# A new slot table behind the attention scores, and a tail whose last batch is finished tile by tile

## The reference

```
def _L0_attn_ref(x, w_in, b_in, w_out, b_out):          # 16 heads of 16
    x_proj = (x @ w_in.T + b_in).reshape(b, l, h, -1)
    q, k, v = jnp.split(x_proj, 3, axis=-1)
    att = jnp.einsum('blhd,bmhd->blmh', q, k) * scale
    att = jax.nn.softmax(att, axis=2)
    opt = jnp.einsum('blmh,blhd->blhd', att, v).reshape(b, l, d)
    return opt @ w_out.T + b_out
...
x = x + _layernorm(_L0_attn_ref(_layernorm(x), ...))
x = x + _layernorm(_L0_ffn_ref(_layernorm(x), ...))
```

## Time and profile before

| what | value |
|---|---|
| median of three runs | 593.8 us (593.7 to 595.99) |
| profiled execution: time, span | 595.68 us, 593.9 us |
| PE, weight loads, DVE, ACT, POOL busy | 519.8, 414.0, 489.3, 466.8, 211.3 us |
| share of the span | 88, 70, 82, 79, 36% |
| exponentials (L358) | 512, idle before them 16.5 us |
| maxima (L499) | 512, idle before them 36.9 us, mostly for PE |
| mean granted clock of PE | 0.94 of full speed |

### The profile page before, as it was taken

How to read it: one execution, slowest core, us unless ns; L and a number is a source line. 1 busy time by engine, 2 the same in 40 slices (tenths; PEclk the granted TensorE clock), 3 DMA queues, 4 the chain that set the end, 5 groups by cost and what they waited for, 6 DMA issues and landing times.

```text
span 593.9 us, 8508 instructions
## 1 busy us (share of the span) xinstructions
PE 519.8 (88%) x2640; PEld 414.0 (70%) x2640; DVE 489.3 (82%) x1025; ACT 466.8 (79%) x1249; POOL 211.3 (36%) x385
## 2 busy tenths in 40 slices
...
GB/s 255 13 238 168 74 117 94 0 130 84 94 13 125 76 55 100 84 70 62 142 24 120 72 108 35 143 71 72 35 140 73 57 54 2 1 36 0 1 36 35
DMA packets 21812, 46.16 MB, mean 78 GB/s; under 512 B 4901, under 2 KB 13221, under 8 KB 21128
## 3 DMA queue, kind: packets, MB, share of 16 engines
...
## 4 chain that ended last, share of the span: by engine, by line
PE 42%; DVE 26%; ACT 21%; POOL 6%; issue 2%; SPq 1%; DMA 0%; POOLq 0%; DVEq 0%; ACTq 0%
PE pu L148 23%; ACT ps L358 16%; DVE nmax L499 14%; PE ps L163 9%; DVE st L529 5%; PE ps L148 4%; POOL y L720 2%; PE pu L168 2%; DVE inter L525 2%; POOL nmr L714 2%; DVE mv L534 2%; ACT inter L421 2%; PE pu L254 1%; ACT vo L378 1%; DVE qk L513 1%
## 5 line engine op out<-in xcount | busy, mean ns | idle before, releaser
L358 ACT ACTIVATE ps<-ps,nmax 128x512 f32<-128x512 f32 x512 | 341.5, 680 | 16.5 <-DVE nmax L499 16.2
L499 DVE TENSOR_REDUCE nmax<-ps 128x1 f32<-128x512 f32 x512 | 322.3, 681 | 36.9 <-PE ps L163 35.9
L163 PE MATMUL ps<-stack 128*128 128x512 f32 x512 | 196.9, 457 | 24.8 <-ACT ps L358 18.5
L163 PEld LDWEIGHTS ps<-stack 128*128 128x128 f32 x512 | 98.5, 203 | 73.8 <-ACT ps L358 55.4
L358 ACT ACTIVATION_READ_ACCUMULATOR ps<-ps,nmax 128x1 f32 x512 | 116.2, 227 | 0.0
L148 PE MATMUL pu<-yT,wi_r 128*128 128x512 f32 x336 | 90.2, 404 | 6.1 <-DVE inter L525 4.8
L148 PEld LDWEIGHTS pu<-wo_r,inter 128*128 128x128 f32 x624 | 80.8, 190 | 5.1 <-DVE qk L513 1.4
L148 PE MATMUL pu<-wo_r,inter 128*128 128x256 f32 x624 | 84.2, 285 | 0.0
L148 PEld LDWEIGHTS pu<-yT,wi_r 128*128 128x128 f32 x336 | 63.0, 191 | 23.1 <-DVE inter L525 6.4
L711 POOL TENSOR_SCALAR nmr<-mv 128x4 f32<-128x4 f32 (+1 forms) x35 | 8.4, 239 | 156.4 <-DVE mv L534 155.8
L734 POOL TENSOR_TENSOR ml<-gs,g 128x128 f32<-128x128 f32 x8 | 3.3, 413 | 146.6 <-DVE g L616 146.6
...
## 6 DMA issues: line engine op xcount, KB each, us to landing
stack<-qk SPq DMA_DIRECT2D x256, 128.0 KB, 2.5
...
```

Of the source, the lines that this page charges most:

```text
L163: e.matmul(ps[i % NS][:], st[:, 1 - p, c, t * 128:(t + 1) * 128], st[:, 2, c, :], start=True, stop=True).then_inc(scored, 1)
L358: e.activation(ps[i % NS][:], ps[i % NS][:], ACT.Exp, bias=nmax[:, i % 8:i % 8 + 1], accum_out=ssum[:, b % 2, t, h:h + 1]).then_inc(exped, 1)
L499: e.tensor_reduce(nmax[:, i % 8:i % 8 + 1], ps[i % NS][:], AX_X, ALU.max, negate=True).then_inc(maxed, 1)
```

## The change

All three slot tables are written anew. In batch b, `f1` units 0 to 2 of batch b - 1 now stand at the end (PE slots 29 to 31), and units 3 to 7 of batch b - 2 at slots 0 to 2, 7 and 8. `masked_t` moves from slot 31 to 28 on PE and from slot 0 of the next batch to slot 28 on ACT. The four projection tiles stand in two slots instead of four; `f2` is split into slots 10 to 13 and 24 to 27; in the last batch (b = 7) it fills slots 9 to 17 instead (`g` and `h` choose: the one that is out of range issues nothing). On Pool `y2_norm` goes ahead of `x_norm`. In the tail five `f1` units of batch 6 are left, two of them behind the projections; Pool does both first passes before both second ones. The last batch's second layer is one unit per tile in a bank of its own, with copy, statistics, norm, add and store tile by tile. The diff, cut to its core (indentation halved; old table lines mostly left out, since they are printed above):

```diff
@@ -97,7 +97,7 @@
 bg_loaded, wout_loaded, lora_loaded, rows_moved = sem("bg_l"), sem("wout_l"), sem("lora_l"), sem("rows_m")
...
 stacked = [sem(f"stacked{i}") for i in range(PIECES)]
-stored = [sem(f"stored{i}") for i in range(XB + 1)]
+stored = [sem(f"stored{i}") for i in range(XB)]
...
@@ -112,6 +112,7 @@
 xnT_high, qk_high, yT_high, f1_high = (sem(n + "_high") for n in ("xnT", "qk", "yT", "f1"))
...
 v_here, oT_here, y_here, gT_here, lt_here, y2_here = (sem(n + "_here") for n in ("v", "oT", "y", "gT", "lt", "y2"))
+f2_tile_ps, y2_tile_here, tile_stored = sem("f2_tile_ps"), sem("y2_tile_here"), sem("tile_stored")
...
@@ -268,6 +269,15 @@
         if k:
...
           filling.clear()
+
+  def f2_last(t):
+
+    bank = banks[take(("f2", B - 1, t), y2_tile_here, t + 1)]
+    if t == 0:
+      e.wait_ge(f1_low, 8 * B)
+    three(bank[:, 0:256], lambda a, f: inter[:, a, f, t * 128:(t + 1) * 128], lambda a, f: wo_r[:, a, f, :],
+       range(8), True, False)
+    e.matmul(bank[:, 0:256], ones_r[:], br_r[:, BW], start=False, stop=True).then_inc(f2_tile_ps, 1)
...
@@ -287,61 +297,62 @@
       e.wait_ge(wout_loaded, 16)
...
       e.wait_ge(lora_moved, 16)
-    slot(0), f1(b - 2, 0)
-    slot(1), f1(b - 2, 1)
-    slot(2), f1(b - 2, 2)
+
+    g, h = (b - 2, B) if b < B - 1 else (B, b - 2)
+    slot(0), f1(b - 2, 3)
+    slot(1), f1(b - 2, 4)
+    slot(2), f1(b - 2, 5)
     slot(3), o_t(b - 1, 0), o_t(b - 1, 1)
-    slot(4), f1(b - 2, 3)
...
-    slot(31), masked_t(b - 1)
+    slot(4)
+    slot(5), project(b - 1, 0), project(b - 1, 1)
+    slot(6), project(b - 1, 2), project(b - 1, 3)
+    slot(7), f1(b - 2, 6)
+    slot(8), f1(b - 2, 7)
+    slot(9), x_t(b + 1, 0), x_t(b + 1, 1), f2(h, 0, 0)
+    slot(10), f2(g, 0, 0), f2(h, 0, 1)
+    slot(11), f2(g, 0, 1), f2(h, 1, 0)
+    slot(12), f2(g, 1, 0), f2(h, 1, 1)
+    slot(13), f2(g, 1, 1), f2(h, 2, 0)
+    slot(14), q_k(b + 1, 0), f2(h, 2, 1)
+    slot(15), q_k(b + 1, 1), f2(h, 3, 0)
+    slot(16), y_t(b - 1, 0), y_t(b - 1, 1)
+    slot(17), q_k(b + 1, 2), f2(h, 3, 1)
+    slot(18), q_k(b + 1, 3)
+    slot(19), gate(b - 1)
+    slot(20), value(b + 1, 0)
+    slot(21), value(b + 1, 1), gate_t(b - 1)
+    slot(22), value(b + 1, 2)
+    slot(23), value(b + 1, 3)
+    slot(24), f2(g, 2, 0)
+    slot(25), f2(g, 2, 1)
+    slot(26), f2(g, 3, 0)
+    slot(27), f2(g, 3, 1)
+    slot(28), masked_t(b - 1)
+    slot(29), f1(b - 1, 0)
+    slot(30), f1(b - 1, 1)
+    slot(31), f1(b - 1, 2)
   b = B - 1
...
     banks.append(ps[i])
-  for f in range(4):
-    f1(b - 1, f)
+  f1(b - 1, 3), f1(b - 1, 4)
   o_t(b, 0), o_t(b, 1)
-  for f in range(4, 8):
-    f1(b - 1, f)
+  f1(b - 1, 5)
   for t in ALL:
     project(b, t)
-  f2(b - 1, 0, 0), f2(b - 1, 0, 1), f2(b - 1, 1, 0), f2(b - 1, 1, 1)
+  f1(b - 1, 6), f1(b - 1, 7)
+  f2(b - 1, 0, 0), f2(b - 1, 0, 1), f2(b - 1, 1, 0)
   y_t(b, 0), y_t(b, 1)
+  f2(b - 1, 1, 1)
+  gate(b)
   f2(b - 1, 2, 0)
-  gate(b)
-  f2(b - 1, 2, 1)
   gate_t(b)
-  f2(b - 1, 3, 0), f2(b - 1, 3, 1)
+  f2(b - 1, 2, 1), f2(b - 1, 3, 0), f2(b - 1, 3, 1)
   masked_t(b)
...
   for t in ALL:
-    f2(b, t, 0), f2(b, t, 1)
+    f2_last(t)
...
@@ -438,56 +449,59 @@
       pair(PAIRS * b + s)
...
       e.wait_ge(bg_loaded, 16)
-    slot(0), masked_t(b - 2)
-    slot(1), f1(b - 2, 0)
-    slot(2), f1(b - 2, 1)
-    slot(3), f1(b - 2, 2)
+    g, h = (b - 2, B) if b < B - 1 else (B, b - 2)
+    slot(0), f1(b - 2, 2)
+    slot(1), f1(b - 2, 3)
+    slot(2), f1(b - 2, 4)
+    slot(3), f1(b - 2, 5)
     slot(4), o_t(b - 1, 0), o_t(b - 1, 1)
-    slot(5), f1(b - 2, 3)
...
-    slot(20)
+    slot(5)
+    slot(6), project(b - 1, 0)
+    slot(7), project(b - 1, 1)
+    slot(8), f1(b - 2, 6)
+    slot(9), f1(b - 2, 7)
+    slot(10), x_t(b + 1, 0)
+    slot(11), x_t(b + 1, 1)
+    slot(12)
+    slot(13), f2(h, 0)
+    slot(14), f2(g, 0)
+    slot(15), q_k(b + 1, 0)
+    slot(16), q_k(b + 1, 1)
+    slot(17), y_t(b - 1, 0), y_t(b - 1, 1)
+    slot(18), q_k(b + 1, 2), f2(h, 1)
+    slot(19), q_k(b + 1, 3)
+    slot(20), gate(b - 1)
     slot(21)
-    slot(22), gate(b - 1)
...
-    slot(28)
+    slot(22), logits(b - 1)
+    slot(23), gate_exp(b - 1)
     if b == 0:
       e.wait_ge(late, 16)
-    slot(29), value(b + 1, 0)
-    slot(30)
-    slot(31), value(b + 1, 1)
+    value(b + 1, 0)
+    slot(24)
+    slot(25), value(b + 1, 1)
+    slot(26)
+    slot(27)
+    slot(28), masked_t(b - 1)
+    slot(29), f2(g, 1)
+    slot(30), f1(b - 1, 0)
+    slot(31), f1(b - 1, 1)
   b = B - 1
-  masked_t(b - 1)
-  for f in range(4):
-    f1(b - 1, f)
+  f1(b - 1, 2), f1(b - 1, 3), f1(b - 1, 4)
   o_t(b, 0), o_t(b, 1)
-  for f in range(4, 8):
-    f1(b - 1, f)
+  f1(b - 1, 5)
   project(b, 0), project(b, 1)
+  f1(b - 1, 6), f1(b - 1, 7)
+  y_t(b, 0), y_t(b, 1)
   f2(b - 1, 0)
-  y_t(b, 0), y_t(b, 1)
   gate(b), logits(b), gate_exp(b)
...
     f1(b, f)
-  f2(b, 0), f2(b, 1)
+  e.wait_ge(added[3], 4 * b)
+  for t in ALL:
+    e.wait_ge(f2_tile_ps, t + 1)
+    e.activation(y2[:, t, :], bank_of["f2", b, t][:, 0:256], ACT.Copy).then_inc(y2_tile_here, 1)
...
@@ -529,7 +543,7 @@
     e.bn_stats(st6[n][:, t, :], src[:, t, :]).then_inc(stats[i], 1)
...
   def whole_stats(i, n, b, ts):
-    e.wait_ge(stats[i], 8 * b + (4 if ts[0] else 0) + len(ts))
+    e.wait_ge(stats[i], 8 * b + 2 * ts[0] + len(ts))
...
@@ -616,7 +630,7 @@
       e.tensor_tensor(g8[:, 5], g8[:, 4], wide(4), ALU.is_equal).then_inc(gated, 1)
...
   def norm(i, n, dst, src, b, ts):
-    e.wait_ge(rstd[i], 3 * b + 3 if ts[0] == 0 else 3 * b + 6)
+    e.wait_ge(rstd[i], 3 * b + 3 + 3 * (ts[0] // len(ts)))
     for t in ts:
...
               ALU.mult).then_inc(normed[i], 1)
@@ -649,56 +663,63 @@
   for b in range(B):
...
       pair(PAIRS * b + s + 1)
-    slot(0), ratio(b - 1)
...
-    f1(b - 2, 2), slot(4)
+    g, h = (b - 2, B) if b < B - 1 else (B, b - 2)
+    f1(b - 2, 1), slot(0), ratio(b - 1)
+    f1(b - 2, 2), slot(1)
+    f1(b - 2, 3), slot(2)
+    f1(b - 2, 4), slot(3), x_stats(b + 1)
+    f1(b - 2, 5), slot(4)
     slot(5)
-    f1(b - 2, 3), slot(6)
...
-    y_t(b - 1, 0), y_t(b - 1, 1), slot(21)
+    slot(6)
+    slot(7), y_stats(b - 1, HALVES[0])
+    slot(8), y_stats(b - 1, HALVES[1])
+    f1(b - 2, 6), slot(9)
+    f1(b - 2, 7), slot(10)
+    slot(11)
+    x_t(b + 1, 0), x_t(b + 1, 1), slot(12), sum_stats(b - 1)
+    slot(13)
+    slot(14), y2_stats(h, HALVES[0])
+    slot(15), y2_stats(g, HALVES[0])
+    slot(16)
+    q_k(b + 1, 0), slot(17)
+    q_k(b + 1, 1), slot(18)
+    y_t(b - 1, 0), y_t(b - 1, 1), slot(19), y2_stats(h, HALVES[1])
+    q_k(b + 1, 2), slot(20)
+    q_k(b + 1, 3), slot(21)
     slot(22)
-    slot(23)
...
-    slot(31)
+    gate_1(b - 1), slot(23)
+    slot(24), gate_2(b - 1)
+    slot(25), gate_3(b - 1)
+    slot(26)
+    slot(27)
+    slot(28)
+    slot(29)
+    slot(30), y2_stats(g, HALVES[1])
+    f1(b - 1, 0), slot(31)
   b = B - 1
+  f1(b - 1, 1)
   ratio(b)
-  for f in range(8):
+  for f in range(2, 6):
     f1(b - 1, f)
   y_stats(b, HALVES[0]), y_stats(b, HALVES[1])
-  for ts in HALVES:
-    norm(1, 1, y, y, b, ts), add(1, y, b, ts)
-    sum_stats(b, ts)
+  norm(1, 1, y, y, b, HALVES[0]), add(1, y, b, HALVES[0])
+  f1(b - 1, 6)
+  sum_stats(b, HALVES[0])
+  f1(b - 1, 7)
+  norm(1, 1, y, y, b, HALVES[1]), add(1, y, b, HALVES[1])
+  sum_stats(b, HALVES[1])
   for ts in HALVES:
...
   gate_1(b), gate_2(b), gate_3(b)
-  y2_stats(b - 1)
+  y2_stats(b - 1, HALVES[0]), y2_stats(b - 1, HALVES[1])
   for f in range(8):
     f1(b, f)
-  y2_stats(b, HALVES[0]), y2_stats(b, HALVES[1])
-  for ts in HALVES:
-    norm(3, 2, y2, y2, b, ts), add(3, y2, b, ts)
+  for t in ALL:
+    e.wait_ge(y2_tile_here, t + 1)
+    tile_stats(3, 2, y2, t)
+    whole_stats(3, 2, b, (t,))
+    norm(3, 2, y2, y2, b, (t,)), add(3, y2, b, (t,))
...
@@ -706,8 +727,8 @@
   def spread(i, n, b, ts=ALL):
...
     s = slice(ts[0], ts[-1] + 1)
-    k = 3 * b + (3 if ts[0] else 0)
-    e.wait_ge(stats[i], 8 * b + 8 if ts[-1] == NT - 1 else 8 * b + 4)
+    k = 3 * b + 3 * (ts[0] // len(ts))
+    e.wait_ge(stats[i], 8 * b + 2 * ts[-1] + 2)
     e.tensor_scalar(nmr[n][:, 0, s], mv[n][:, s, 0], -1.0, None, ALU.mult).then_inc(rstd[i], 1)
...
     e.wait_ge(rstd[i], k + 2)
@@ -812,19 +833,21 @@
   e.wait_ge(late, LATE)
...
     scale(b - 1)
+    y2_norm(b - 3)
     x_norm(b + 1)
-    y2_norm(b - 3)
     y_norm(b - 1)
     sum_norm(b - 1)
+    if b == B - 1:
+      y2_norm(b - 2)
     mask(b - 1)
...
   scale(b)
-  y2_norm(b - 2)
-  spread(1, 1, b, HALVES[0]), spread(2, 1, b, HALVES[0])
-  spread(1, 1, b, HALVES[1]), spread(2, 1, b, HALVES[1])
+  spread(1, 1, b, HALVES[0]), spread(1, 1, b, HALVES[1])
+  spread(2, 1, b, HALVES[0]), spread(2, 1, b, HALVES[1])
   mask(b)
   y2_norm(b - 1)
-  spread(3, 2, b, HALVES[0]), spread(3, 2, b, HALVES[1])
+  for t in ALL:
+    spread(3, 2, b, (t,))
...
@@ -888,13 +911,12 @@
     stacks(b + 1, 0), stacks(b + 1, 1), stacks(b + 1, 2)
...
   b = B - 1
-  for i, (t, n) in enumerate(((2, slice(0, 2)), (4, slice(2, 4)))):
```

(22 more changed lines are left out.)

58 lines of the change are left out of this document (1 added, 57 removed).

## The result

| what | before | after |
|---|---|---|
| median (nine runs each, same chip) | 595.06 us (593.7 to 595.99) | 599.34 us (595.92 to 600.4) |
| profiled execution: time, span | 595.68, 593.9 us | 595.92, 594.1 us |
| PE, DVE, ACT, POOL busy | 519.8, 489.3, 466.8, 211.3 us | 522.6, 491.3, 465.6, 212.9 us |
| mean granted clock of PE | 0.94 | 0.94 |

The ratio is 1.0077, with a 95% interval from 1.0061 to 1.0094: slower by 0.8%. Predicted were 589.3 us and a gain; the time lies in the upper end of the range that was given.

What follows compares the result with a forecast made beforehand. No single engine was taken as the bound, but the order of work on PE, DVE and ACT, coupled by bank hand-over. Terms +3.3 +2.0 -1.0 -8.8 = -4.5 against the median of 593.8 gave 589.3 us, range 575.5 to 600.

Steps and rivals of the forecast that it cites:

- the one on the clock: PE's light work in slots 3 and 4: one clock fall costs 2.5 us, but none was counted in steady batches.
- the second rival: Clock falls in slots 3 and 4 of each steady batch, slowing projections and f1: 5 x 2.5, 601.8 us; chance 0.12.
- The second mis-sized term: Batch 1 receives three f1 units: +2.0 us, from 0 (all under ACT) to +5 (units in full).
- batch 7, to the last exponential: PE bounds its first part, ACT the second; 59.2 us where it was 60.2: -1.0, between -2.5 and +1.
- tail: From the last exponential to the end, 75.1 us before: -8.8, between -6 and -11.
- The walk of the steady batch: Batches 2 to 6, stepped through with unit prices and bank hand-overs: 63.6 us against 62.9, +0.65 each, +3.3 in all.
- The `lt_ps` wait: After pair 28, ACT waits 2.2 us for PE to write that bank; PE loses 1.3 us.
- The wait for pair 7's bank: Slots 3 and 4: DVE's low parts and x statistics delay pair 5's maxima, so PE loses 2.5 us.
- the first three parts: After the last exponential: to the second projection copy -6.6, to y's transposes -1.7, to the last low part -0.8 us.
- the order smooths the load: Steady batches: no yT stall and f2 split, so DVE loses 3 us a batch: 61.2 each, 576 in all; chance 0.20.
- the wait before the copy passes on in full: ACT's wait before `lt_ps` costs 2.2 us instead of 1.3: +4.5, 593.8 us; chance 0.20.
- the tail isn't PE's: After the last exponential, the chain of reciprocal, scaling, transposes and norms sets the time; half of 8.8 gone: 593.7 us; chance 0.06.

Runs made afterwards that it cites:

- the repeat: The changed kernel run and profiled again with no edit: 599.2 us, ratio 1.0087.
- the fill: Changed kernel with repeated score matmuls: at pairs 6 and 7 from batch 2 on, 595.55 us; for batch 1's 2.7, late in batches 1 and 7, 596.64 us.
- both fills: Changed kernel with extra score matmuls in pairs 6 and 7 of batches 2 to 7 and in late pairs of batches 1 and 7: 592.39 us, ratio 0.9968.
- the move: Changed kernel with the copy `lt_r` one slot later on ACT, behind pair 29's exponentials instead of pair 28's: 589.6 us.
- two small moves: Changed kernel with x statistics behind slot 5 and `lt_r`'s copy one slot later, run together with the last second layer in two halves: 580.43 us.
- a third: Kernel with x statistics and `lt_r` later and last second layer halved, plus f1(6) from PE slot 7 to 4 and f1(7) from 8 to 7: 576.99 us.
- the split end: Changed kernel with only f2_last split into two halves of four chunks, the first waiting for four low parts only: 598.07 us.
- batches 1 and 7 filled: Changed kernel with score matmuls issued twice in pairs 24 to 30 of batch 1 and 20 to 30 of batch 7: 596.64 us.
- the first fill: Changed kernel with both matmuls of pair 6 and the first of pair 7 issued four times each from batch 2 on: 595.55 us.
- the move of the statistics: Changed kernel with DVE's x statistics behind slot 5 instead of slot 3 from batch 1 on: 593.03 us, ratio 0.9989.

## Why the prediction was wrong

**The step that failed** is the one on the clock. The prediction worked out the second rival's mechanism at the right place (slots 3 and 4, the projections behind them at 1.2 GHz), and gave it a chance of 0.12 because "in this trace no steady batch shows it"; the forecast's own sum has nothing for it in the steady batches. The kernel before has no such stretch, so its steady batches could not show it; what counted was that its trace held a stretch that fell and one that didn't, which is no evidence for none in five. Measured: 1.6 us a fall instead of 2.5, in three of five batches (in the repeat too), 4.8 and 4.9 us in the two traces and 3.65 us of the median by the fill. The Trainium skill (TensorE: Matmul & The Clock Gate, section on a second HAM failure mode) tells of a kernel whose matrix unit idles briefly between groups of matmuls as its banks go round, and whose clock swings for it. The trace agrees, with its waits of 1.70 us on a score bank and no DMA in them, but for one thing: identical batches with identical waits fell in one case and not in the other.

**The second mis-sized term** is batch 1. It was put at +2.0 with 1.5 of clock in it. It came out at +3.9 in one profiled execution and +6.5 in the other, and still at +3.8 with the clock filled up. The 3.8 is what is left after the wait for Pool before y's transposes is gone (1.57 us in batch 1 before), so the three units cost near their full price (the bound of +5) and have little of the cover by ACT that was assumed. The copy `lt_r`, which stands in front of them, is part of it: moving it gave batch 1 back 3.7 us against the repeat, but only 1.0 (59.7 to 58.7) against the kernel whose clock was filled up there. The slow clock adds up to 2.7 more, by the fill.

**The terms in one table**, from profiled spans. The column at full clock is the kernel with both fills, against the kernel before.

| term | predicted | after | after, both fills |
|---|---|---|---|
| batch 0 and start | 0 | -2.4 | -0.2 |
| batch 1 | +2.0 | +3.9 | +3.8 |
| batches 2 to 6 | +3.3 | +9.2 | +4.4 |
| batch 7, to the last exponential | -1.0 | -0.4 | -2.0 |
| tail | -8.8 | -10.1 | -10.1 |
| sum | -4.5 | +0.2 | -4.1 |

The last column is the forecast at full clock. That its sum comes within 0.4 us is luck twice over. Misses of 1.8 in batch 1 and 1.1 in the steady ones are met by 2.3 in batch 7 and the tail. And the two traces flatter the change: 595.68 us is a long execution of the kernel before, with two falls in its batch 7, and 591.61 a short one of the filled kernel. By the ratio of their runs (0.9968) the gain at full clock is 1.9 us, between 1.0 and 2.8, and not 4.1; without the falls, about 2 of the forecast's 4.5 us were there. The start of the profiled execution of after was 2.4 us early; in the repeat it was 0.4, batch 1 was 62.4, and the sum +5.3, nearer to the medians' +4.3.

**Point by point.** The walk of the steady batch was right in kind and size: 63.6 forecast, 63.9 at full clock, so +0.9 to +1.0 a batch where +0.65 was counted. It holds at its stations too (PE timeline; zero is PE's pair in slot 9):

```profile
293.73 0.63 PE L164 MATMUL ps<-stack 128*128 128x512 f32 x2
...
330.25 0.48 PE L164 MATMUL ps<-stack 128*128 128x512 f32 x1
...
344.31 0.63 PE L164 MATMUL ps<-stack 128*128 128x512 f32 x2
```

The pair behind slot 28's transposes starts at 36.5 (walked 36.4), slot 3 begins at 50.6 (50.3), and pair 7's bank comes at 55.0 (54.8; the matmul at 348.69 above). The last stretch was summed a little short: four projection tiles, two f1 units and four pairs are 9.0 us by the prediction's own prices, not 8.8, and took 8.9. The `lt_ps` wait was forecast at 2.2 us on ACT and 1.3 on PE, measured 2.37 and 1.12 by row and 1.4 by the move. The wait for pair 7's bank was walked at 2.5 us lost; the rows show 1.70 and 0.17 just before, of which only 0.5 to 0.6 belonged to the statistics. No wait on Pool stands before y's transposes in a steady batch. In the tail the first three parts are within 0.2 us each, and the slow clock behind the gap before y's transposes is gone, as forecast (the eight took 1.94 us before and 1.06 after). The last was forecast at +0.35 and came at -0.65: the wait was right (1.50 for 1.55), but the smaller last piece saves more, of which 0.4 is the store (1.7 us for 128 KB, 2.1 for the 256 KB of before on the page's part 6), for which I had counted nothing (and a gain of at most 0.5 allowed). Alone on the old kernel this edit is worth nothing that can be measured.

**The other rivals.** That the order smooths the load (61.2 a batch) did not happen with this table, but it was nearer than it looked: two small moves bring it to 61.9 and a third to 61.4. That the wait before the copy passes on in full (2.2) is refuted by the 1.4. That the tail isn't PE's is refuted by the first part's -6.6.

**What stays open** is what decides in which batches the clock falls. With the same instructions it was 3, 5, 6 in one execution, 2, 4, 6 in another, and in kernels whose edits lie elsewhere 4 and 5 (the split end) and 3 and 5 (batches 1 and 7 filled). Nothing was tried on it. That light work on PE ahead of the projections makes the fall possible is shown by the first fill, which adds work there and takes the falls away, and agrees with the move of the statistics, which shortens the wait. Open, too, is how often the kernel before has its falls in batch 7.
